# Value products with nine weight columns in place of thirty-two

## The reference

```
scores = einsum('bhqd,bhkd->bhqk', q, k) / sqrt(8)
w      = relu(scores)
attn   = w / (sum(w, axis=-1) + 1e-6)
out    = einsum('bhqk,bhkd->bhqd', attn, v)        # 16 heads x 8 columns
x      = x + layernorm(norm(x) + out @ w_out + b_out) * gamma + beta
x      = x + sqrt((norm(x) @ cos(theta + n1))**2 + (norm(x) @ sin(phi + n2))**2)
```

## Time and profile before

| | |
|---|---|
| median of 3 runs | 420.01 us (419.9 to 420.16) |
| span of the profiled execution | 417.7 us |
| between the two | 2.3 us |
| TensorE matmuls (PE) busy | 410.0 us, 98%, 3261 instructions |
| TensorE weight loads (PEld) busy | 117.6 us, 28%, 3261 instructions |
| VectorE (DVE) busy | 330.6 us, 79% |
| ScalarE (ACT) busy | 341.1 us, 82% |
| GpSimd (POOL) busy | 49.4 us, 12% |

### The profile page before, as it was taken

One profiled execution on the slowest core, in us unless ns is written; L12 is line 12 of the kernel. 1 busy time (PEld: TensorE's weight loads), 2 busy tenths in 40 slices (PEclk: granted clock), 3 DMA queues, 4 the chain that ended last, 5 costly groups with the idle time before them and its releaser, 6 DMA issues.

```text
span 417.7 us, 8994 instructions
## 1 busy us (share of the span) xinstructions
PE 410.0 (98%) x3261; PEld 117.6 (28%) x3261; DVE 330.6 (79%) x652; ACT 341.1 (82%) x611; POOL 49.4 (12%) x57
## 2 busy tenths in 40 slices
PE   8999999999999999999999999999999999999995
PEld 5333222222223222322222322222222322222234
DVE  6877878887888888678778888677778788767856
ACT  4879888887888898788888798888887798879864
POOL 2004000079301000000301000000100000000111
PEclk9999999999999999999999999999999999999999
DMA  5117831010031101001021100001012000000200
GB/s 170 46 51 147 173 92 52 2 27 26 4 93 30 50 2 32 22 0 53 27 65 43 52 2 20 31 2 53 27 50 58 2 25 2 27 2 27 68 2 25
DMA packets 11741, 17.54 MB, mean 42 GB/s; under 512 B 3684, under 2 KB 5364, under 8 KB 11316
## 3 DMA queue, kind: packets, MB, share of 16 engines
q1 hardware_dynamic: 11556, 16.84, 15.0%
q10 hardware_dynamic: 144, 0.13, 0.2%
HBM read 3.99 MB, written 5.11 MB: 22 GB/s over the span
## 4 chain that ended last, share of the span: by engine, by line
PE 95%; DVE 2%; DMA 1%; ACT 0%; issue 0%; SPq 0%; DVEq 0%
PE pv L1163 61%; PE sc L1128 27%; PE pv L1221 2%; PE pv L1054 1%; PE pv L1063 1%; DMA wqkv_sb<-w_qkv_dram 1%; PE pv L1075 1%; PE pv L1189 1%; PE pv L1170 0%; PE sc L1221 0%; DVE x L978 0%; PE pv L1043 0%; PE sc L1170 0%; PE sc L1276 0%; DVE x L996 0%
## 5 line engine op out<-in xcount | busy, mean ns | idle before, releaser
L1163 PE MATMUL pv<-w_buf,v_sb 128*32 128x512 f32 x2048 | 272.3, 604 | 0.0
L783 DVE TENSOR_SCALAR w_buf<-sc 128x512 f32<-128x512 f32 x256 | 176.8, 691 | 69.4 <-PE sc L1128 59.8
L603 ACT ACTIVATE w_buf<-sc 128x512 f32<-128x512 f32 x256 | 153.1, 598 | 61.4 <-PE sc L1128 60.9
L611 ACT ACTIVATE w_buf<-sc 128x512 f32<-128x512 f32 (+1 forms) x254 | 183.5, 722 | 0.0
L1128 PE MATMUL sc<-q_rep,k_rep 32*128 32x512 f32 x1024 | 132.3, 494 | 0.2 <-DVE k_rep L756 0.2
L790 DVE TENSOR_SCALAR w_buf<-sc 128x512 f32<-128x512 f32 x180 | 123.4, 686 | 0.0
L1128 PEld LDWEIGHTS sc<-q_rep,k_rep 32*128 32x128 f32 x1024 | 51.0, 181 | 214.1 <-ACT w_buf L603 178.0
L1163 PEld LDWEIGHTS pv<-w_buf,v_sb 128*32 128x32 f32 x2048 | 40.4, 108 | 66.6 <-ACT w_buf L611 36.9
L494 POOL TENSOR_TENSOR oT<-o_raw,o_scale 128x512 f32<-128x512 f32 (+1 forms) x4 | 5.1, 1281 | 84.7 <-issue 60.7
L500 POOL TENSOR_TENSOR x<-x,mv 128x512 f32<-128x512 f32 (+1 forms) x5 | 4.3, 869 | 75.4 <-DVE x L891 63.0
L510 POOL TENSOR_TENSOR mag<-sq 128x256 f32<-128x256 f32 x6 | 4.4, 730 | 69.8 <-ACT sq L650 69.8
(11 more groups left out here) (132 smaller groups left out, 148.5 us busy)
## 6 DMA issues: line engine op xcount, KB each, us to landing
pv_dram<-pv_sb SPq DMA_DIRECT2D x15, 256.0 KB, 2.0
q_rep<-q_hi SPq DMA_DIRECT2D x30, 64.0 KB, 2.1
q_rep<-q_lo SPq DMA_DIRECT2D x30, 64.0 KB, 2.1
k_rep<-k_hi SPq DMA_DIRECT2D x6, 256.0 KB, 4.1
k_rep<-k_lo SPq DMA_DIRECT2D x6, 256.0 KB, 5.4
x_sb<-x_dram SPq DMA_DIRECT2D x3, 256.0 KB, 4.3
o_raw<-pv_dram SPq DMA_DIRECT2D x3, 256.0 KB
o_scale<-inverse_dram SPq DMA_DIRECT2D x3, 256.0 KB
```

Of the source, the lines that this page charges most:

```text
L603: nc.scalar.activation(w_buf[:, s % W_STEPS, 0, :], early[:, 0, :], ACT.Relu).then_inc(relu[0], 2 if none else 1)
L611: nc.scalar.activation(w_buf[:, s % W_STEPS, 2:2 + n, :], late[:, 0:n, :], ACT.Relu).then_inc(relu[0], 1)
L783: nc.vector.tensor_scalar(w_buf[:, s % W_STEPS, 1, :], early[:, 1, :], 0.0, None, ALU.max).then_inc(relu[1], 2 if both else 1)
L1163: last = nc.tensor.matmul(bank[32 * i:32 * i + 32, :], v_sb[:, k, HPG * g + i, :], w_buf[:, s % W_STEPS, i, :], start=(k == 0), stop=(k == ...
```

## The change

The four value products of a step name fewer columns and fewer rows. As weights they take columns 0 to 8 of a head's 32 in `v_sb`, and they write partitions 32 i to 32 i + 8 of the bank, where they wrote 32 i to 32 i + 31.

```
--- before.py
+++ after.py
@@ -1160,7 +1160,7 @@
                     for i in range(HPG):
-                        last = nc.tensor.matmul(bank[32 * i:32 * i + 32, :], v_sb[:, k, HPG * g + i, :],
+                        last = nc.tensor.matmul(bank[32 * i:32 * i + HD + 1, :], v_sb[:, k, HPG * g + i, 0:HD + 1],
                                                 w_buf[:, s % W_STEPS, i, :], start=(k == 0), stop=(k == NT - 1))
```

## The result

| | median us | lowest to highest |
|---|---|---|
| before | 419.95 (4 runs) | 419.34 to 420.16 |
| after | 416.01 (4 runs) | 415.7 to 416.15 |

The ratio is 0.9911, with a 95% interval of 0.9897 to 0.9924: 3.7 us less than before by the ratio, 3.9 by the medians. The forecast was 3.1 us less, 416.9.

A forecast was written before the change was run, and what follows sets the result against it. TensorE bounds the kernel; 417.7 us of span less 4.80 for shorter exposed loads plus 1.66 given back to ReLU waits is 414.6, with 2.3 around it 416.9 us. The range was 415.0 to 420.1, the mechanism's own 415.0 to 418.5.

The forecast's parts named there:

- The bound: Whole kernel: TensorE is 95% of the chain that ends last; a step of 1.43 us, 256 times, is 366 us.
- The exposed load: First wave of value matmuls behind scores: 23 fewer weight columns save 18.9 ns in each of 254 steps, 4.80 us.
- The argument for a column count under 32: Transpose loads, 140 ns with 128 columns and 90 with 16: load time follows the used columns within a 32-column tile.
- The rule that loads are pulled ahead of matmuls: Value loads: by the skill's rule all would be hidden, the change worth 0; by the trace's rows it is worth 4.80 us.
- Fewer rows written: Value matmuls' output: 32 and 128 rows both take 592 ns at the least, so saving 23 rows gives 0.
- The give-back: Late scores waiting for the early ReLU of the step before: 88 places by 18.9 ns return 1.66 us.
- the 76 steps: Steps where ACT takes both late banks: L783 begins 0.07 us later, so they already wait and lose the 18.9 ns.
- 12 other places: Estimated places with epilogue pieces between the ReLUs, such as at 168, each also waiting 18.9 ns longer.
- the term of 2.3 us around the span: Time outside the span: 2.3 us added to the 414.6 us span to give 416.9.
- No change: Value loads: not shortened or not exposed, so 420.0 us; chance 0.10.
- the ReLU path binding everywhere: Ordinary steps too: spare time under 0.06 us, so most gain is waited away, 418.5 to 419.3 us; chance 0.04.
- slower by a nine-column load off the fast path: First wave of value steps: odd-count load exposes 105 ns instead of 25, 20.3 us more, 440; slower has chance 0.05.

The follow-up runs named there:

- doubled kernels: Each step's eight value matmuls made twice in a row: 636.89 us on the kernel before (32 columns), 632.09 us with nine columns.
- coarse counts: Kernels before and after as they stand: DVE's early ReLU adds 2 where ACT takes both late banks; 419.95 us before, 416.01 us after.
- exact counts: Every ReLU adds 1 to its semaphore and TensorE waits for the number really reached: 414.54 us on the changed kernel, 418.83 us on the kernel before.
- without the padding: GpSimd's memsets of the 23 unused columns and their waits removed from the nine-column kernel whose ReLUs each add 1: 414.70 us, ratio 0.9878.

## Why the prediction was right

- **The bound.** TensorE sets the end. The chain after is 96% TensorE, and the beat of a step fell where TensorE's own load fell.
- **The exposed load, 18.9 ns by 254 steps, 4.80 us.** Right in place and size. The usual first-wave matmul fell by 19 to 20 ns (617 to 597 or 598), and the doubled kernels, where nothing else is due, stand 4.8 us apart by the medians and 4.9 by the value matmuls.
- **The argument for a column count under 32.** The conclusion was right, but the transposes of the earlier trace rows didn't show it. The 0.446 ns a column and the fixed 83 ns were worked out from the 90 ns of the 16-column load, so that 83 + 7 gives 90 says nothing. With 73 ns fixed and 0.52 a column the same two rows fit a tile that is always loaded as 32 columns. What settles it are the runs with 16, nine and one columns, 95, 90 and 82 ns, all under the 109 of 32.
- **The rule that loads are pulled ahead of matmuls.** The trace showed it for a value step behind a value step and not behind scores, and the doubled kernel shows both in one step: 617 ns in the first loop, 593 in the second. The Trainium skill's "TensorE: Matmul & The Clock Gate", section "Step-by-step: what each phase is for", ties the pull-ahead to row groups that don't conflict or to the background weight buffer, and the trace agrees for value loads behind value matmuls, whose matmuls take 592 or 593 ns. Which of the two conditions fails behind the scores no run here shows.
- **Fewer rows written, 0.** Right: the shortest matmul is 592 ns with 128, 32, 16 and nine rows.
- **The give-back, 1.66 us.** The total was right, and the split partly luck. 4.9 less the 3.3 us of the first to the last value matmul is 1.6. The prediction had all of the 76 steps at the limit, 1.44 us, and 12 other places, 0.23. By the starts of the late halves, less the 7 ns that are no wait, the waits behind the 76 grew from 1.35 to 2.38 us, so 1.0 us, since only 58 of them waited before and 60 after; and those elsewhere grew from 1.36 to 1.77 us, 0.4, in some 20 places. Too much in one and too little in the other nearly cancel. The last 0.1 to 0.2 us is open. The cause named, L783 starting late in the 76 steps, was shown by taking it away: with nine columns 2.5 us came back, about the 2.38 that these steps waited, the part from before the change included. Of the 2.38, 0.78 are in the two steps where L783 was 0.42 us late. What the count has to do with that delay is open; it was there in every profile with coarse counts and a single value loop, and in none with exact ones.
- **What the sum lacked.** The forecast of 416.9 is 0.9 us over the 416.0 measured. Of that, 0.2 lie in the steps (3.3 us less for 3.14) and 0.3 in the start-up of the two profiled executions, which the change doesn't touch; in the profiles of nine columns the first value matmul starts anywhere from 14.1 to 15.2 us. The remaining 0.4 is the term of 2.3 us around the span. It was the median less the span of one profiled execution, and within one execution the two are 1.8 to 1.9 us apart in every run of either kernel that lists both. So the profiled execution of the kernel before was about 0.5 us faster than its median, and 2.3 is too much.
- **The rivals.** No change fell with the measured time, the ReLU path binding everywhere with ordinary steps of 1.41 to 1.42 us for 1.43, and slower by a nine-column load off the fast path with loads of 90 ns, on the line of the others. The granted clock is full in all slices after as before.

## What to carry to other kernels

A weight load costs time only where it can't be pulled ahead, and a matmul's usual length in the exposed place less its shortest shows how much of it is exposed. Name as weights there only the columns that are used. Before counting a saving, look which group already starts at the least distance behind its releaser: those steps give the saving back. A count from the schedule is an upper bound for them, 76 here, of which about 60 waited. The cheapest further gain was not on the bounding engine but in the semaphore amount of the one behind it: nine columns with exact counts are the fastest version here, with or without the padding: 414.5 us, 1.2% under the kernel before.

## What the runs showed of the hardware that was not expected

- DVE's ReLU starts 0.07 us later where it adds 2 to a semaphore than where it adds 1 (202.49 against ACT's 202.42, and 202.38 for both with exact counts). ACT's L603 does it too in the two steps in which it adds 2: 0.60 us behind the scores, and 0.54 with exact counts. That the amount goes with the delay is shown. It isn't the only thing that does: in 14 other steps L783 adds 1 and starts 0.07 us late as well, in the same steps before and after the change, and in 20 with exact counts. Why, perhaps a wait that is then an instruction of its own, is only argued.
- With one weight column a matmul of 512 columns takes 590 to 592 ns and its load 82: a load has a fixed part as long as over 90 columns' worth, and no matmul is longer for it, not even behind another kind of product.
